# The last block's latent loop: steps written out, one head with four tiles a product, output sums turned feature by token

## What is computed

```python
xn = _l2norm(x, d) * gamma_norm
q = (xn @ Wq_w + Wq_b).reshape(b, s, G, H, DQK)          # 8 groups of 16 heads
...
kc = jnp.einsum('bsd,bsl->bld', k, w).reshape(b, L, G, DQK)   # L = 100 latents
vc = jnp.einsum('bsd,bsl->bld', v, w).reshape(b, L, G, DV)
qk = jnp.einsum('bsghd,blgd->bghsl', q, kc) * (1.0 / DQK ** 0.5)
att = jax.nn.softmax(qk, axis=-1)
z = jnp.einsum('bghsl,blgd->bsghd', att, vc).reshape(b, s, G * H * DV)
zn = _l2norm(z, G * H * DV) * wz_g1
h1 = jax.nn.silu(zn @ wz_w1 + wz_b1)                     # 256 features
h1n = _l2norm(h1, 2 * FF) * wz_g2
out = jax.nn.silu(h1n @ wz_w2 + wz_b2)
```

## Time and profile before

| | us |
|---|---|
| median of 3 executions (3467.41 to 3475.9) | 3473.49 |
| the profiled execution | 3499.97 |
| its span, first to last instruction | 3498.2 |
| TensorE busy in it | 3053.3 |
| VectorE, ScalarE, GpSimd busy | 2413.0, 1801.3, 1773.0 |

### The profile page before, as it was taken

One profiled execution on the slowest core, in us unless ns is written; L12 is line 12 of the kernel. 1 busy time (PEld: TensorE's weight loads), 2 busy tenths in 40 slices (PEclk: granted clock), 3 DMA queues, 4 the chain that ended last, 5 costly groups with the idle time before them and its releaser, 6 DMA issues.

```text
span 3498.2 us, 57433 instructions
## 1 busy us (share of the span) xinstructions
PE 3053.3 (87%) x18996; PEld 2673.3 (76%) x19032; DVE 2413.0 (69%) x4368; ACT 1801.3 (51%) x3135; POOL 1773.0 (51%) x1524
## 2 busy tenths in 40 slices
PE   1556666668999999879999999999799999999997
PEld 1434445457788888759999999999699999999986
DVE  1456766643677676657777777777577777777774
ACT  0256666523666565525555555555455555555544
POOL 5466656500200000126666666666366666666663
PEclk9879999969999999979999999999899999999997
DMA  1010000000000000010000000000000000000010
GB/s 41 32 25 18 19 13 18 7 25 21 13 0 0 0 0 0 11 50 28 27 27 27 27 27 27 27 27 28 17 28 27 27 27 27 27 27 27 27 34 7
DMA packets 36972, 75.92 MB, mean 22 GB/s; under 512 B 9644, under 2 KB 13876, under 8 KB 36120
## 3 DMA queue, kind: packets, MB, share of 16 engines
q1 hardware_dynamic: 35352, 71.68, 6.5%
q0 software_dynamic: 1536, 3.15, 0.3%
HBM read 65.36 MB, written 1.05 MB: 19 GB/s over the span
## 4 chain that ended last, share of the span: by engine, by line
PE 47%; issue 5%; POOL 3%; DVE 1%; ACT 0%; POOLq 0%; DVEq 0%; ACTq 0%
PE lat_ps_h L1837 19%; PE lat_ps_z L1851 9%; PE lat_ps_s L1763 7%; PE lat_ps_t L1790 6%; PE lat_ps_z L1781 3%; POOL lat_zz L1570 2%; PE lat_ps_z L1773 2%; PE lat_ps_z L1861 1%; POOL latm_wq L1549 0%; POOL latm_wq L1543 0%; POOL latm_att L1562 0%; POOL latm_vcg L1554 0%; PE lat_ps_s L1879 0%; DVE latm_norm L1669 0%; DVE latm_h L1675 0%
## 5 line engine op out<-in xcount | busy, mean ns | idle before, releaser
L1837 PE MATMUL lat_ps_h<-latm_share,latm_attT 100*128 100x256 f32 x6144 | 886.8, 286 | 0.1
L1837 PEld LDWEIGHTS lat_ps_h<-latm_share,latm_attT 100*128 100x128 f32 x6144 | 818.7, 189 | 24.9 <-DVE latm_attT L1626 11.8
L1562 POOL TENSOR_TENSOR latm_att<-latm_sc,latm_tot 128x400 f32<-128x400 f32 x516 | 441.3, 855 | 617.7 <-DVE latm_tot L1621 588.1
L1570 POOL TENSOR_TENSOR lat_zz<-lat_zz,lat_zsq 128x512 f32<-128x512 f32 x514 | 660.3, 1285 | 0.3
L1698 ACT ACTIVATE latm_sc<-latm_sc 128x400 f32<-128x400 f32 x516 | 279.1, 541 | 430.8 <-DVE latm_sc L1612 430.8
L1851 PE MATMUL lat_ps_z<-latm_attT,latm_vg 100*128 100x512 f32 x1536 | 485.8, 424 | 0.0
L1619 DVE TENSOR_REDUCE latm_tot<-latm_sc 128x4 f32<-128x400 f32 x516 | 291.3, 565 | 157.4 <-ACT latm_sc L1698 157.4
L533 POOL TENSOR_TENSOR ret_probs<-ret_probs,ret_shared 128x1024 f32<-128x1024 f32 x128 | 305.7, 2389 | 181.4 <-ACT ret_probs L666 181.4
L1626 DVE TENSOR_TENSOR latm_attT<-lat_ps_t,latm_attT 100x512 fp32r<-100x512 f32 x514 | 349.8, 681 | 61.7 <-ACT latm_attT L1714 61.7
L1714 ACT CAST latm_attT<-lat_ps_t 100x512 fp32r<-100x512 f32 x514 | 301.0, 586 | 147.3 <-PE lat_ps_t L1790 123.1
L1763 PE MATMUL lat_ps_s<-latm_wk,lat_xr 128*128 128x400 f32 x1548 | 368.8, 347 | 3.0 <-issue 3.0
(11 more groups left out here) (339 smaller groups left out, 5012.4 us busy)
## 6 DMA issues: line engine op xcount, KB each, us to landing
lat_w_in<-in_w_quads SPq DMA_DIRECT2D x65, 512.0 KB, 3.6
lat_wq_in<-in_wq_quads SPq DMA_DIRECT2D x65, 256.0 KB, 2.6
ret_qk_head<-ret_qk_parts SPq DMA_DIRECT2D x256, 32.0 KB, 2.0
moe_w<-in_W SPq DMA_DIRECT2D x2, 1024.0 KB
mha_wqk<-in_Wqk SPq DMA_DIRECT2D x1, 1152.0 KB, 5.6
ret_shared<-in_xpos_q SPq DMA_DIRECT2D x1, 1024.0 KB, 5.3
ret_shared<-in_xpos_k SPq DMA_DIRECT2D x1, 1024.0 KB, 5.0
latw_wkv<-in_Wkv SPq DMA_DIRECT2D x1, 1024.0 KB
```

What stands on the lines that cost most here:

```text
L1562: nc.gpsimd.tensor_tensor(att[:, u].rearrange("p (j l) -> p j l", j=QH), sc[:, u].rearrange("p (j l) -> p j l", j=QH), tot[:, u].unsqueeze ...
L1570: nc.gpsimd.tensor_tensor(zz[:, t], zz[:, t], zsq[:, u], ALU.add).then_inc(s["zz_added"], 1)
L1837: mm = e.matmul(ps_h[:, t, :], attT[:, t % 2, a_part, j * P:(j + 1) * P], share[:, u, w_part, j * FF2:(j + 1) * FF2], start=False, stop=Fa ...
```

## The change

All of it lies in `latent`.

- The hardware loops are gone: one Python loop over n = -6 ... 519 writes out every step for each engine, both batches in one row of K = 512 steps, with constant counts to wait for. Scores, subtraction, exponentials and `weight` run LEAD = 6 steps ahead (k = n + 6), in a ring of eight tiles `att` (SLOTS), in place of two.
- `turn` takes one head of four tiles, not four heads of one tile: step n (j = n % 4) handles head j of the half batch of four tiles. attT then has 512 tokens in its columns. In `add` a 128-column piece of `share` is the loaded operand and attT streams 512 columns: six products into `ps_h[:, f, half]`, feature by token. No products of zeros; `start` and `stop` stand at a batch's first and last product. `reduce_heads` (z) reads `vc` itself; the copy `vg` is gone.
- The next `wk` and `share` are made in the bank of `ps_s` that holds no scores just then (`spare_bank`), behind a wait for the subtraction of the scores before, ahead of the step's `add`; the next scores into that bank wait until the low part is taken (`free_spare`).
- On VectorE `total` takes the tile before (k - 1), and `mean_wq` stands behind `low`. On ScalarE `high` stands ahead of `exponentials`. On GpSimd `centre_wq` comes one step later than `mean_wq` and `weight` ahead of `add_squares`. SyncE loads quad q when the weights of q - 2 are scaled and its share made.
- The end of a batch is cut in two units of 512 tokens and in stages, each with its step in MIDDLE or ENDING. Those of batch 0 lie among the steps of batch 1, the scratch products in the free score bank. zz holds one 128 x 1024 sum a batch, so the norm is 8 passes a unit. Its inverse root is spread over partitions (GpSimd multiplies it into the identity, TensorE multiplies ones by that) and multiplied into hT by VectorE, feature by token, so there are no transposes. Roots are `inverse_root` on VectorE: a first guess by integer shift and three Newton steps, one of the four a step in batch 0's units, two or four a step at the end. Silu is tanh on ScalarE and a product (`gate`, `finish`) on VectorE. The stores are one a unit.
- In the phase's first half GpSimd no longer clears `zero`, the ends of kcT and vcT, `zz` and `zsq`; a small `mean_col` is set.

The diff, cut to its core:

```diff
+            makes_wk = lambda n: (n + LEAD) % TB == 5 and 0 <= (n + LEAD) // TB + 1 < B * NQ
+            makes_share = lambda n: n % TB in (4, 5) and 0 <= n // TB + 1 < B * NQ
+            units = [(b, c) for b in range(B) for c in range(2)]
...
+            def spare_bank(n):
+                return ps_s[:, (n + LEAD + 1) % 2]
...
+                for n in range(-LEAD, END):
+                    k = n + LEAD
+                    if 1 <= k <= K:
+                        weight(k - 1)
+                    if 1 <= n <= K:
+                        add_squares(n - 1)
+                    if n % TB == 1 and 0 <= quad(n) + 1 < B * NQ:
+                        scale_vc(quad(n) + 1)
+                    if n == -LEAD:
+                        scale_vc(0)
+                    if k % TB == 0 and quad(k) + 1 < B * NQ:
+                        scale_wq(quad(k) + 1)
+                    if k % TB == 3 and quad(k) + 1 < B * NQ:
+                        centre_wq(quad(k) + 1)
+                    for i, b, c in due(n, "spread"):
+                        spread_norm(i)
...
+                def inverse_root(which, step, floor, done):
+                    x, y = sums[:, which], inv[:, which]
+                    if step == 0:
+                        c.then(e.tensor_scalar(x, x, floor, None, ALU.max))
+                        c.then(e.tensor_scalar(y.bitcast(I32), x.bitcast(I32), 1, None, ALU.logical_shift_right))
+                        c.then(e.tensor_scalar(y.bitcast(I32), y.bitcast(I32), -1.0, float(0x5f3759df), ALU.mult, ALU.add))
+                    else:
+                        c.then(e.tensor_tensor(newton[:], y, y, ALU.mult))
+                        c.then(e.tensor_tensor(newton[:], newton[:], x, ALU.mult))
+                        c.then(e.tensor_scalar(newton[:], newton[:], -0.5, 1.5, ALU.mult, ALU.add))
+                        c.then(e.tensor_tensor(y, y, newton[:], ALU.mult))
+                    if step == STEPS - 1:
+                        e.sem_inc(s[done], 1)
...
+                def scale_h(i, half, bank):
+                    e.wait_ge(s["wide_ready"], START + i + 1)
+                    e.wait_ge(s["h_kept"], START + 2 * i + 2)
+                    for f in range(2):
+                        c.then(e.tensor_tensor(hT[:, half, f], bank, hT[:, half, f], ALU.mult))
+                    e.sem_inc(s["h_scaled"], 1)
+                    for f in range(2):
+                        last = e.tensor_scalar(hT[:, half, f], hT[:, half, f], b1[:, f:f + 1], None, ALU.add)
+                    last.then_inc(s["h_biased"], 1)
...
+                for n in range(-LEAD, END):
+                    k = n + LEAD
+                    if k < K:
+                        shift(k)
+                    if makes_wk(n):
+                        low_wk(quad(k) + 1, spare_bank(n))
+                    if makes_share(n):
+                        low_share(quad(n) + 1, n % TB - 4, spare_bank(n))
...
+                    if 1 <= k <= K:
+                        total(k - 1)
+                    if 0 <= n + 1 < K:
+                        low(n + 1)
+                    if k % TB == 2 and quad(k) + 1 < B * NQ:
+                        mean_wq(quad(k) + 1)
...
+                    for i, step in rooting(n, "root"):
+                        root_of_norm(i, step)
...
+                def free_spare(n):
+                    if makes_wk(n):
+                        e.wait_ge(s["wk_ready"], START + quad(n + LEAD) + 2)
+                    if makes_share(n):
+                        e.wait_ge(s["share_ready"], START + 2 * (quad(n) + 1) + n % TB - 4 + 1)
...
-                def make_wk(count, row):
-                    e.wait_ge(s["wq_ready"], START + count + 1)
+                def make_wk(q, bank):
+                    e.wait_ge(s["wq_ready"], START + q + 1)
                     for j in range(QH):
-                        mm = e.matmul(ps_z[:, j * L:(j + 1) * L], wq[:, j, :], kcT[:, bass.ds(row, 1), :].rearrange("p a l -> p (a l)"),
-                                      start=True, stop=True)
+                        mm = e.matmul(bank[:, j * L:(j + 1) * L], wq[:, j, :], kcT[:, row(q), :], start=True, stop=True)
                     mm.then_inc(s["wk_made"], 1)
...
-                def turn(k, u, b):
-                    e.wait_ge(s["weighted"], START + b * (NS + 2) + k + 1)
-                    e.wait_ge(s["attT_ready"], START + b * (NS + 1) + k)
-                    for j in range(QH):
-                        mm = e.transpose(ps_t[0:L, j * P:(j + 1) * P], att[:, u, j * L:(j + 1) * L], ident[:])
+                def turn(n):
+                    half, j = n % TB // 4, n % 4
+                    if j == 0:
+                        e.wait_ge(s["weighted"], START + n + 4)
+                    e.wait_ge(s["attT_ready"], START + n)
+                    for i in range(4):
+                        mm = e.transpose(ps_t[0:L, i * P:(i + 1) * P], att[:, (n - j + i) % SLOTS, j * L:(j + 1) * L], ident[:])
...
-                                for a_part, w_part in ((0, 0), (0, 1), (1, 0)):
-                                    if a_part == 1:
-                                        e.wait_ge(s["attT_ready"], START + b * (NS + 1) + k + 1)
-                                    for j in range(QH):
-                                        if (a_part, w_part, j) == (0, 0, 2) and t in (3, 4, 5):
-                                            e.wait_ge(s["squared"], START + n)
-                                            if t == 3:
-                                                make_wk(quad_next, row)
-                                            else:
-                                                make_share(quad_next, t - 4, load, u1)
...
-                                        mm = e.matmul(ps_h[:, t, :], attT[:, t % 2, a_part, j * P:(j + 1) * P],
-                                                      share[:, u, w_part, j * FF2:(j + 1) * FF2],
-                                                      start=False, stop=False, skip_group_check=True)
...
+                def add(n):
+                    q, half, j = quad(n), n % TB // 4, n % 4
+                    if n % TB == 0:
+                        e.wait_ge(s["share_ready"], START + 2 * q + 2)
+                    if n % NS in (0, 4) and n >= NS:
+                        e.wait_ge(s["h_kept"], START + 2 * half + 2)
+                    e.wait_ge(s["attT_high"], START + n + 1)
+                    for a_part, w_parts in ((0, (0, 1)), (1, (0,))):
+                        if a_part == 1:
+                            e.wait_ge(s["attT_ready"], START + n + 1)
+                        for f in range(2):
+                            for w_part in w_parts:
+                                cols = slice(j * FF2 + f * P, j * FF2 + (f + 1) * P)
+                                mm = e.matmul(ps_h[:, f, half, :], share[:, q % 2, w_part, cols], attT[:, n % 2, a_part],
+                                              start=(n % NS in (0, 4) and (a_part, w_part) == (0, 0)),
+                                              stop=(n % NS in (NS - 5, NS - 1) and a_part == 1), skip_group_check=True)
+                    mm.then_inc(s["added"], 1)
+                def reduce_heads(n):
+                    e.wait_ge(s["squared"], START + n)
+                    for i, (v_part, a_part) in enumerate(PARTS):
+                        mm = e.matmul(ps_z[:], vc[:, v_part, row(quad(n))], attT[:, n % 2, a_part], start=(i == 0), stop=(i == 2))
+                    mm.then_inc(s["z_ready"], 1)
...
+                make_wk(0, ps_s[:, 1])
+                for n in range(-LEAD, END):
+                    k = n + LEAD
+                    if n - 1 >= -LEAD:
+                        free_spare(n - 1)
+                    if k < K:
+                        score(k)
+                    if makes_wk(n):
+                        e.wait_ge(s["shifted"], START + k)
+                        make_wk(quad(k) + 1, spare_bank(n))
+                    if makes_share(n):
+                        e.wait_ge(s["shifted"], START + k)
+                        make_share(quad(n) + 1, n % TB - 4, spare_bank(n))
+                    if n < K - LEAD:
+                        if any(due(n, stage) for stage in ("norm", "wide", "power", "result")):
+                            e.wait_ge(s["shifted"], START + k)
+                        tail(n)
+                    if 0 <= n < K:
+                        add(n)
+                    if 0 <= n + 1 < K:
+                        turn(n + 1)
+                    if 0 <= n < K:
+                        reduce_heads(n)
+                    if n >= K - LEAD:
+                        e.wait_ge(s["shifted"], START + K)
+                        tail(n)
```

(16 more changed lines are left out.)

593 lines of the change are left out of this document (299 added, 294 removed).

## The result

| | before | after |
|---|---|---|
| median of the runs, us | 3470.45 (3465.01 to 3475.9) | 3363.36 (3361.44 to 3366.82) |
| ratio | | 0.9696 (95% interval 0.9679 to 0.9713) |
| the profiled execution, its span | 3499.97, 3498.2 | 3361.44, 3359.7 |
| latent loops and ends, from the first `wk` product to the end | 1946.6 | 1839.9 |

The two profiled executions stand 138 us apart, 29 of it in phases that the change does not touch: the first L142 starts at 121.2 us in the one and at 92.5 in the other.

The account below looks back on a forecast made before the run. TensorE, 99% busy in the latent loops, was taken as the bound. Start 20 + steps 1788.8 + middle 35 + end 32.6 - memsets 1.7 = 1874.7 against 1946.7; 72 us off gave 3401, range 3375 to 3452.

Parts of the forecast that it names:

- the quad: Eight steps of the latent loop: predicted 28.05 us, against 28.64 in the first loop before.
- lower bound: Least time forecast for eight loop steps, with no wait: 27.85 us; the upper bound was 28.85.
- two share halves: TensorE work in two of eight steps: 1.05 us each, read from the cleaner share step.
- wait for `centre_wq`: GpSimd, in the step making the next weights: ready some 0.2 us after TensorE asks, once per eight steps.
- the stall and its clock dip: Second loop, before L1763 at 3336.67: 3.0 us stall plus about 1.7 for the lower clock, gone with the loops.
- 28.72: Old time in us for eight loop steps, averaged over both loops; 0.7 of it was taken as waiting.
- The middle: Batch 0's end work among batch 1's steps: 35 us (11 TensorE, 18 roots, 6 rest), bounds 12 and 50.
- Start, end, memsets: Latent phase: start about 20 us, not 16.3; end 32.6, not 45.7; GpSimd's memsets gone before it, -1.7.
- The quads did not keep their waits: Rival, chance 0.2: late `mean_wq` and `centre_wq` cost what today's waits do, 28.6 us per eight steps, total 3436.
- The roots did not slip past GpSimd: Rival, chance 0.15: roots slip past GpSimd, batch 0's end work costs 17 not 35, the end 29; total 3380.
- Written-out code was not late: Rival, chance 0.05: code written out in place of loops arrives late, kernel slower; 3551 with a third of 96 blocks stalling.
- The case that the change does little: Rival, chance 0.05: eight steps stay at 28.6, batch 0's end work costs 50, the end 40; total 3458.

Follow-up runs that it names:

- with reciprocals: Changed kernel with each of batch 0's Newton instructions replaced by a reciprocal of the same four columns at the same place; ratio 0.9648 to the kernel before.
- ahead of `total`: Changed kernel with batch 0's Newton steps moved ahead of `total` on VectorE; ratio 0.9667 to the kernel before.

## Why the prediction was wrong

**The term that failed is the quad.** I had 28.05 us and a lower bound of 27.85; it is 27.31. Times 64 that is 47 us, more than the whole miss of 35. By its parts:

| per quad | predicted | measured | 
|---|---|---|
| eight plain steps | 8 x 3.09 = 24.72 | 8 x 3.08 = 24.64 |
| two share halves | 2 x 1.05 = 2.10 | 2 x 0.86 = 1.72 |
| `wk` | 1.03 | 0.89 |
| wait for `centre_wq` | 0.20 | 0.06 |
| sum | 28.05 | 27.31 |

Half of it is the share half. I had read it from the "cleaner" of the two share steps of the earlier trace rows, 4.16 less 3.105, and taken that as free of waits. It was not: the run that adds only the free score bank to the written-out loops brings both share steps to 3.98 and 3.94, some 0.86 above a plain step, and four share passes 0.215 us apart are 0.86. Likewise I took 0.2 of waiting off the `wk` step and it held more: eight passes of 100 columns start 0.112 us apart, 0.89 in all. So my lower bound, 27.85, had waits in it: with everything else at its best, a forecast built on it ends at 3401 - 13 - 21 = 3367. TensorE's busy share of 99% did not show this: a wait in mid-product of 0.1 to 0.2 us is hidden in the modelled ends of the matmuls before it. Distances between starts do show it.

**What the old quad's waits were**, from the runs: 28.60 before; 0.11 goes with the loops; 0.54 with the bank, all of it in the two share steps; 0.29 is the second step, 3.37 and now 3.07, whose wait came from `mean_wq`; 0.23 is the `wk` step, 4.26 to 4.03, mostly the wait for `centre_wq`; 0.12 is left, of which 0.07 is the width of the passes. In the second step the twelve products of the kernel before took 1.84 us, not 1.58: the ninth, the first to read attT's low part, waited for it.

```profile
2405.18 1.84 PE L1837 MATMUL lat_ps_h<-latm_share,latm_attT 100*128 100x256 f32 x12
```

It is not the place behind the low part that removed this wait, for with `mean_wq` back between subtraction and total the quad is 27.25. What is left is the step that it falls in, now one with a share half, and the longer lead. The 0.29 and the 0.23 are read from the steps and traces; the lead was not varied by itself, since gathering four tiles for one turn needs it.

**`centre_wq`.** I had it 0.2 us late. It ends at 2003.50, where the first `wk` pass starts at 2003.69, 0.18 behind the last score pass as ever; only the second pass comes 0.12 to 0.16 behind the first, not 0.085. With `mean_wq` early it ends 0.78 us ahead of that pass, and the quad is 0.06 shorter.

**Loops.** I took the stall and its clock dip as part of 28.72 and nothing more. The stall was 4.5 us, as priced; the loops cost some 7.5 us besides, 0.11 a quad, for which I had no term.

**The middle** was right in mechanism and nearly in size: the nine quads of the third window are 285.43 us, and 285.43 - 9 x 27.31 = 39.6 where I had 35. Four quads of 34.4 to 35.3 us carry most of it, those with the roots; with reciprocals they take 28.9 to 29.9. So the roots cost 21.7 us, 5.4 a group: my own sum (5.5 for each of four groups, 22) was right, and taking 18 in its place, because some of L1633's cases had not waited, was not. The 17.9 left agree with the 11 + 6 for the rest. The three Newton steps of a group are not 4 to 5 us each as I had said, but 4.5 to 4.6, 6.0 to 7.6 and 4.2 to 5.8, two of them with a share half in the same step.
By the rule of the Trainium skill ("SBUF — State Buffer", "Who interferes with whom", which ops grab the shared pair) every root step waits and the roots cost 22 to 30 us; 21.7 was measured, just under that. Not every instruction waited: all 12 of L1719, the last of each step, kept to 163 ns in the mean.

**Start, end, memsets.** The start is 21.1 us (20 predicted), the end 34.3 (32.6). L143 did lose its memset:

```profile
L143 DVE TENSOR_SCALAR lat_stat<-lat_stat x1: 175/175/175, 1452.5 to 1452.5; 128x16 f32<-128x16 f32 x1
```

1.91 us became 0.175, but the time from the start of L142 to the first `wk` product only went from 69.80 to 69.58: L1411 then waited 1.42 us for TensorE's L1303. The 1.7 us did not come.

**The sum.** 21.1 + 1784.5 (first product to last head sum; predicted 1788.8 + 35 = 1823.8) + 34.3 = 1839.9, against 1876.4 without the memsets' 1.7. The quad gives -47, the middle +5, the rest of the steps, start and end +6. That start, end and middle all came out above their terms, and the memsets' 1.7 not at all, took some 13 us off the miss; that is luck.

**The rivals.** The quads did not keep their waits (28.6); they lost more than the forecast's. The roots did not slip past GpSimd. Written-out code was not late, in 101 blocks. The case that the change does little is out.

## What to carry to other kernels

A floor for a step is not the shortest step of its kind in the trace, if every step of that kind holds the same wait: add it up from the distances between starts of its passes, and compare with a step that has no such wait. A bank that two chains share costs on both sides, so a product put later in the step moves the wait and does not remove it. Before an instruction is moved in one engine's order, follow what then stands behind it in the next engine's queue; behind the low part `mean_wq` (1.65 us) cost TensorE 0.78 us in the next step by way of ScalarE's fixed order, while in a longer step, with the copy ahead of the exponential, it costs 0.06 a quad. Where two waits end at nearly the same time, taking one away shows nothing; look for the second before the first is called worthless. And small VectorE instructions of the kinds below belong where GpSimd is waiting, not where it runs.

## What the runs showed of the hardware that I had not expected

- Small VectorE instructions on SBUF differ: a 128x4 TENSOR_TENSOR lasted 1208 ns on average where all of them met GpSimd's and 718 ahead of `total`, where 8 of 12 did, TENSOR_SCALAR 722 against 170, SCALAR_TENSOR_TENSOR 831 against 162, while 32 RECIPROCALs in the same places kept to 173.
- Such a VectorE instruction ends with the GpSimd instruction that it meets, whatever its own size: L1717 at 2453.41, L1634 at 2453.38, and the same within 0.03 us for all 20 of L1717 and L1718 that met one and for 63 of 64 of `mean_wq`'s L1695 in the changed kernel (the one that met none took 164 ns).
- A distance between starts across a change of form must be read together with the one behind it. Transposes start 0.108 us apart and passes of 512 columns 0.233; at the change the first long pass starts only 0.028 behind the last transpose and the second 0.316 behind the first, 0.344 in all, which is 0.108 + 0.233 within 0.003. Behind the share passes (0.215 apart) it is 0.028 + 0.420, again their sum; behind the `wk` passes (0.112) it is 0.054 + 0.316, 0.025 more than the sum. Both kernels have it alike.
